# A three-layer interaction network with gathered embeddings: scales without rounding to powers of two, and embedding gathers spread two to a step

## The reference

```python
B, F, E = (1024, 48, 32)
LAYER_SIZES = [128, 128, 128]

def _cin_layer(xi, x0, W, b):
    Fi, F0 = (xi.shape[1], x0.shape[1])
    Wr = W.reshape(Fi, F0, -1)
    out = jnp.einsum('nie,nje,ijo->noe', xi, x0, Wr) + b[None, :, None]
    return jax.nn.relu(out)
```

## Time and profile before

| | us |
|---|---|
| median of 3 runs | 2438.37 |
| lowest and highest of them | 2435.81, 2439.48 |
| the profiled execution, its own time | 2440.96 |
| its span, from first to last instruction | 2439.2 |
| PE busy | 2319.3 (95%) |
| DVE busy | 2267.9 (93%) |
| ACT busy | 2115.5 (87%) |
| POOL busy | 1954.1 (80%) |

### The profile page before, as it was taken

The page is one execution under the profiler, slowest core; times in us unless marked ns, Lnnn a source line. Parts: engine busy times, 40 slices in busy tenths (PEclk is TensorE's granted clock), DMA queues, the critical chain, the costliest instruction groups (busy, mean ns, idle before and its releaser), DMA issues.

```text
span 2439.2 us, 68108 instructions
## 1 busy us (share of the span) xinstructions
PE 2319.3 (95%) x14174; PEld 1183.7 (49%) x14174; DVE 2267.9 (93%) x9416; ACT 2115.5 (87%) x7910; POOL 1954.1 (80%) x2134
## 2 busy tenths in 40 slices
PE   1699999999999999999999999999999999999999
PEld 0355455454455454555445544544445555555453
DVE  6499999999999999999999999999999999999995
ACT  4589889888889889889889889889889999999895
POOL 7588888888888888888888888888777777777774
PEclk6799999999999999999999999999999999999999
DMA  5133333333333333333333333333333333333331
GB/s 170 28 72 70 64 70 71 64 68 71 61 71 71 64 68 71 68 66 69 68 65 70 70 71 63 70 71 66 65 70 68 69 63 71 69 69 71 69 70 30
DMA packets 150185, 168.19 MB, mean 69 GB/s; under 512 B 111940, under 2 KB 115655, under 8 KB 150120
## 3 DMA queue, kind: packets, MB, share of 16 engines
q0 software_dynamic: 42864, 136.87, 30.1%
q1 hardware_dynamic: 107256, 30.73, 5.8%
HBM read 12.82 MB, written 0.00 MB: 5 GB/s over the span
## 4 chain that ended last, share of the span: by engine, by line
PE 30%; POOL 18%; issue 16%; ACT 13%; DMA 11%; DVE 9%; DVEq 1%; SPq 1%; ACTq 1%; POOLq 0%
PE y L509 25%; DMA work<-work 10%; ACT work L623 8%; DVE acc L843 5%; POOL part L355 5%; PE m L499 3%; POOL part L359 3%; POOL part L357 3%; POOL emb L300 2%; ACT work L653 2%; POOL psum L362 2%; POOL rest L347 1%; POOL work L332 1%; DVEq L96 1%; ACT zh L651 1%
## 5 line engine op out<-in xcount | busy, mean ns | idle before, releaser
L509 PE MATMUL y<-whi,xT 128*128 128x512 f16 x6144 | 2000.5, 380 | 39.8 <-DVE acc L843 34.0
L623 ACT ACTIVATE work<-y,xc 128x128 f32<-128x128 f32 x5632 | 1610.0, 419 | 182.5 <-PE y L509 158.2
L843 DVE SCALAR_TENSOR_TENSOR acc<-y,xc,acc 128x128 f32<-128x128 f32 x5632 | 1657.6, 346 | 32.0 <-PE y L509 26.3
L509 PE MATMUL y<-wlo,xT 128*128 128x512 f16 x3072 | 1165.6, 379 | 0.0
L509 PEld LDWEIGHTS y<-whi,xT 128*128 128x128 f16 x6144 | 599.3, 98 | 679.9 <-issue 73.6
L509 PEld LDWEIGHTS y<-wlo,xT 128*128 128x128 f16 x3072 | 300.9, 98 | 230.3 <-issue 0.7
L355 POOL TENSOR_TENSOR part<-work 128x512 f32<-128x512 f32 x255 | 324.5, 1272 | 84.4 <-DMA work<-work 68.7
L384 POOL TENSOR_TENSOR zl<-work,zh 128x1152 f16<-128x1152 f32 x128 | 343.3, 2682 | 8.1 <-ACT work L653 8.1
L332 POOL DMA_DIRECT2D work<-work x255 | 229.1, 898 | 111.4 <-ACT work L623 110.2
L343 POOL TENSOR_TENSOR part<-work 128x512 f32<-128x512 f32 x128 | 164.4, 1284 | 133.0 <-ACT work L623 132.9
L300 POOL DMA_INDIRECT emb<-tbl,ids_sb x192 | 202.0, 1052 | 46.7 <-issue 44.2
(11 more groups left out here) (108 smaller groups left out, 2098.8 us busy)
## 6 DMA issues: line engine op xcount, KB each, us to landing
work<-work POOLq DMA_DIRECT2D x255, 512.0 KB, 4.8
xT<-hi SPq DMA_TRANSPOSE x256, 2.2
xT<-lo SPq DMA_TRANSPOSE x256, 2.2
emb<-tbl,ids_sb POOLq DMA_INDIRECT x192, 2.5
xx<-w SPq DMA_DIRECT2D x4, 768.0 KB
work<-w SPq DMA_DIRECT2D x4, 768.0 KB
x0T<-x0hl SPq DMA_TRANSPOSE x128, 2.2
wt_sb<-W_top SPq DMA_DIRECT2D x1, 768.0 KB
```

Of the source, the lines that this page charges most:

```text
L509: ins = nc.tensor.matmul(dst[:], xT[layer][:, parity, a, :], w[layer][:, cols], start=i == 0, stop=i == 2)
L623: nc.scalar.activation(prods[layer][:, a, k * P:(k + 1) * P], bank[:, k * P:(k + 1) * P], ACT.Copy, scale=xc[layer][:, parity, j:j + 1]).t ...
L843: ins = nc.vector.scalar_tensor_tensor(dst, y, col, mine, ALU.mult, ALU.add)
```

## The change

It has three parts.

1. **Scales.** The exponent masking is left out, so that scales are no longer powers of two: `scale` becomes two instructions (`tot`, `sc`) and `x0_scale` three. ACT reads `tot` where it read `mpw`. The factor `wpow` is put into the embeddings themselves when they are spread: `tensor_copy` becomes `tensor_scalar` with `wpow`, on DVE for block 0 and on POOL for the others. ACT's `mpsq` divides it out again with `scale=winv`.
2. **Layout.** In `mx0` the maximum and the clipped maximum of a tile now stand side by side, so the instructions on the two tiles read and write with a stride of two elements.
3. **Gathers.** From step 1 on every step has two gathers, until step 68, where the 144 are given out. The spreads stand in steps 21 to 24, 45 to 48 and 69 to 72.

```diff
-SPREAD, GROUP, EARLY = 8, 12, 8
+SPREAD, GROUP = 8, 12
-SCALE = 4
+SCALE, SCALE0 = 2, 4
...
-                pool.tensor_copy(xx[:, t0:t0 + n, :], src).then_inc(s_xx, n)
+                pool.tensor_scalar(xx[:, t0:t0 + n, :], src, wpow[:, 0:1], None, ALU.mult).then_inc(s_xx, n)
...
-                if v > 0 and (parity == 1 or v <= EARLY):
+                if v > 0:
                     next_gather()
...
-                nc.scalar.activation(mpsq[:], mp0[:], ACT.Square).then_inc(s_mpsq, 2)
+                nc.scalar.activation(mpsq[:], mx0[:, :, 1], ACT.Square, scale=winv[:, 0:1]).then_inc(s_mpsq, 2)
...
-                wait(act, s_scale[l], t * SCALE + 4)
+                wait(act, s_scale[l], (t + 1) * SCALE)
...
-                                     ACT.Copy, scale=mpw[l][:]).then_inc(s_xc[l], 1)
+                                     ACT.Copy, scale=tot[l][:, 1:2]).then_inc(s_xc[l], 1)
...
-                    nc.vector.tensor_scalar(mx0[:, 1, :], mx0[:, 0, :], TINY0, HALF_RANGE, ALU.max, ALU.mult).then_inc(s, 1)
-                elif i == 2:
                     wait(dve, s, done + 2)
                     wait(dve, s_msq, t)
-                    nc.vector.tensor_scalar(mp0[:].bitcast(u32), mx0[:, 1, :].bitcast(u32), EXPONENT, None,
-                                            ALU.bitwise_and).then_inc(s, 1)
-                else:
+                    nc.vector.tensor_scalar(mx0[:, :, 1], mx0[:, :, 0], TINY0, HALF_RANGE, ALU.max, ALU.mult).then_inc(s, 1)
+                elif i == 2:
                     wait(dve, s, done + 3)
                     wait(dve, s_xs0, t)
-                    nc.vector.reciprocal(sc0[:], mp0[:]).then_inc(s, 1)
+                    nc.vector.reciprocal(sc0[:], mx0[:, :, 1]).then_inc(s, 1)
...
                 elif i == 1:
                     wait(dve, s, done + 1)
-                    nc.vector.tensor_scalar(mp[l][:].bitcast(u32), tot[l][:, 1:2].bitcast(u32), EXPONENT, None,
-                                            ALU.bitwise_and).then_inc(s, 1)
-                elif i == 2:
-                    wait(dve, s, done + 2)
                     wait(dve, s_hi[l], t)
-                    nc.vector.reciprocal(sc[l][:], mp[l][:]).then_inc(s, 1)
-                else:
-                    wait(dve, s_xc[l], t)
-                    nc.vector.tensor_scalar(mpw[l][:], mp[l][:], wpow[:, 0:1], None, ALU.mult).then_inc(s, 1)
+                    nc.vector.reciprocal(sc[l][:], tot[l][:, 1:2]).then_inc(s, 1)
```

More of the change, by code:

```diff
@@ L74 @@
 TINY = 1e-30
-TINY0 = 1e-15
+TINY0 = 1e-20
 EXPONENT = 0x7F800000
@@ L120, in build @@
         mx0, sc0 = sb("mx0", [P, 2, 2]), sb("sc0", [P, 2])
-        mp0, mpsq, msq = sb("mp0", [P, 2]), sb("mpsq", [P, 2]), sb("msq", [P, 2])
+        mpsq, msq = sb("mpsq", [P, 2]), sb("msq", [P, 2])
         whi = [sb(f"whi{l}", [P, F * P], f16) for l in (2, 3)]
@@ L144, in build @@
         tot = [sb(f"tot{l}", [P, 2]) for l in (1, 2)]
-        mp = [sb(f"mp{l}", [P, 1]) for l in (1, 2)]
-        mpw = [sb(f"mpw{l}", [P, 1]) for l in (1, 2)]
         sc = [sb(f"sc{l}", [P, 1]) for l in (1, 2)]
@@ L386, in x0_scaled @@
             def x0_scaled(t):
-                wait(pool, s_x0, t * 2 + SCALE)
+                wait(pool, s_x0, t * 2 + SCALE0)
                 wait(pool, s_x0lo, t)
@@ L786, in spread @@
                 fields = slice(g * GROUP, (g + 1) * GROUP)
-                return nc.vector.tensor_copy(xx[:, e0:e1, fields], emb[:, 0, fields, e0:e1].rearrange("p f e -> p e f"))
+                return nc.vector.tensor_scalar(xx[:, e0:e1, fields], emb[:, 0, fields, e0:e1].rearrange("p f e -> p e f"),
+                                               wpow[:, 0:1], None, ALU.mult)
             for g in range(F // GROUP - 1):
@@ L801, in x0_scale @@
                     wait(dve, s_xx, t + 2)
-                    nc.vector.tensor_reduce(mx0[:, 0, :], xx[:, bass.ds(t, 2), :], axis=AX.X, op=ALU.max,
-                                            apply_absolute_value=True).then_inc(s, 1)
+                    nc.vector.tensor_reduce(mx0[:, :, 0], xx[:, bass.ds(t, 2), :], axis=AX.X, op=ALU.max,
+                                            apply_absolute_value=True).then_inc(s, 2)
                 elif i == 1:
-                    wait(dve, s, done + 1)
-                    nc.vector.tensor_scalar(mx0[:, 1, :], mx0[:, 0, :], TINY0, HALF_RANGE, ALU.max, ALU.mult).then_inc(s, 1)
-                elif i == 2:
                     wait(dve, s, done + 2)
                     wait(dve, s_msq, t)
-                    nc.vector.tensor_scalar(mp0[:].bitcast(u32), mx0[:, 1, :].bitcast(u32), EXPONENT, None,
-                                            ALU.bitwise_and).then_inc(s, 1)
-                else:
+                    nc.vector.tensor_scalar(mx0[:, :, 1], mx0[:, :, 0], TINY0, HALF_RANGE, ALU.max, ALU.mult).then_inc(s, 1)
+                elif i == 2:
                     wait(dve, s, done + 3)
                     wait(dve, s_xs0, t)
-                    nc.vector.reciprocal(sc0[:], mp0[:]).then_inc(s, 1)
+                    nc.vector.reciprocal(sc0[:], mx0[:, :, 1]).then_inc(s, 1)
             def stacked_lo(t):
@@ L871, in scale @@
                     wait(dve, s_relu[l], t + 1)
+                    wait(dve, s_xc[l], t)
                     nc.vector.tensor_scalar(tot[l][:, 1:2], tot[l][:, 0:1], TINY, HALF_RANGE, ALU.max,
@@ L920, in step @@
                             pre1(t1, parity)
-                        if n == 7 and active(t1):
+                        if n == 7 and k < SCALE and active(t1):
                             scale(0, t1, k)
@@ L935, in step @@
                             stacked_lo(t1 + 1)
-                        if n == 23 and active(t2):
-                            scale(1, t2, k)
+                        if n == 23 and k in (1, 3) and active(t2):
+                            scale(1, t2, k // 2)
                     if n == 14 and isinstance(v, int) and TILES - 3 - NB * PIECES <= v < TILES - 3:
```

## The result

| kernel | median us | lowest to highest | ratio to before, 95% interval |
|---|---|---|---|
| before | 2438.18 | 2435.81 to 2439.48 | |
| changed | 2422.43 | 2420.61 to 2422.9 | 0.9936, 0.9921 to 0.9951 |

The change takes off 15.8 us; 10.5 were forecast. The profiled execution of the changed kernel took 2422.4 us.

What follows compares the result with a forecast made beforehand. PE was taken to set the pace without gathers (35.36 us a pair), a 36.22 us loop with them; terms -7.7 + 3.0 - 2.7 - 3.6 + 1.2 - 0.7 = -10.5 us gave 2427.9 us, range 2410 to 2440.

Steps and rivals of the forecast that it cites:

- Fewer steps with gathers: Gathers end at step 68, not 88; ten pairs fall to PE's pace, 0.77 us each: -7.7 us.
- A second gather in even steps: Even steps 10 to 68, between `x0_scaled` and `sum_rest(0)`: 30 added gathers at 0.1 us, +3.0 us; bounds 0 and 0.14.
- the cover: POOL's wait for ACT ahead of `sum_rest(0)`, 1.64 us, hides the added gather, with 0.42 us left.
- second rival: If ACT comes over 0.42 us earlier against POOL, the even-step gather is exposed: 37 us more, 2462 us; chance 0.08.
- The earlier release of `hi_part`: ACT's wait for `mpw` shrinks: 0.08 us in each of 34 gather pairs, -2.7 us; bounds 0 and 0.19 us.
- L810 and `mpw` in spread steps: Six even steps with a spread, where DVE's instructions are uncovered: 0.6 us saved each, -3.6 us; bounds nothing and -8.4.
- the spreads' multiplication: POOL's twelve spreads as `tensor_scalar` instead of copy: +0.1 us each, +1.2 us in all; bounds 0 and +19 us.
- Start and end: Scale chains at the first and last tiles have no cover, so shorter scales save there: -0.7 us.
- The loop: Gather stage, closing once a pair through POOL, DVE, PE, ACT: 36.22 us; only shortening its terms shortens the pair, until 35.36.
- POOL's leg: From `add_by_dma(1)` to the end of `psum`: 17.52 us, 16.35 without gathers; the gather behind `squares_lo` makes the difference.
- Its signs: Named trace marks: gather-stage pairs of 36.1 to 36.2 us, POOL's ACT wait about 0.4, spreads 0.9 to 1.1 us.
- The full opening: DVE savings count in full and the gather stage runs at PE's pace: 42 us less, 2396 us; chance 0.1.

Runs made afterwards that it cites:

- e2: Changed kernel with the gathers as before (two and one by turns behind step 8), so scales and spreads alone: 2423.82 us, ratio 0.9938.
- e1: Kernel before with two gathers in every step from step 1 on and nothing else: 2429.7 us, ratio 0.9959.
- e6: Kernel before with one wait moved: layer 1's `hi_part` waits for the third scale instruction, not the fourth: 2429.61 us, ratio 0.9964.
- e3: Changed kernel with POOL's spreads as plain copies, leaving out `wpow` on blocks 1 to 3: 2416.02 us, ratio 0.9901.
- e5: Changed kernel, but behind step 8 the gather behind `squares_lo` is given out in odd steps alone: 2423.09 us, ratio 0.9931.
- e10: Changed kernel with block 1 gathered at the start, then one gather a step, ahead of `sum_rest(0)`, from step 1 on: 2458.94 us, one execution.
- e7: Changed kernel with four small DVE instructions a step put back, writing to a tile nobody reads or waits for: 2422.31 us, ratio 0.9935.

## Why the prediction was right, and where it was not

**The two parts together.** By the terms, the scales with their spreads were to give 5.8 us and the gathers 4.7, together 10.5. Alone they gave 16 (e2) and 10 (e1), and both at once 15.8. Both were forecast too low, by 10 and by 5 us, and they overlap by 10 us, which the sum, where each term stands as if alone, left out. The forecast lies as near as it does because the overlap took back most of what the terms lacked. That is luck.

**Fewer steps with gathers (-7.7 us).** With the old scales -11.3 us (e1, one profile), with the new ones -4.2, since there a pair is worth 0.40 and not 0.77 us.

**A second gather in even steps (+3.0 us).** With the old scales 0 (e1), the lower bound, and the cover was as described. With the new ones 4.6 us, of which the terms on ACT gave no sign: ACT was to gain 0.19 us at most, and the 0.43 us of wait that e1 shows are gone in the changed kernel. So the second rival's condition came, but not its price of 37 us: POOL waits for the adding DMA behind the gather anyway, so 0.15 us a gather was paid and not 1.24, about what that DMA's later landing takes.

**The earlier release of `hi_part` (-2.7 us).** The mechanism was right and the size too small. The release alone gives 0.18 us a pair (e6) where 0.08 was taken, 7.5 us in all. The 1.25 us of the stage without gathers were taken as ACT's own time, and they contained a wait: the same stretch takes 1.01 us once `hi_part` does not wait. The bound of 0.19 us, the idle time shown, was also too small for ACT's stretch, which fell by 0.32: back to back, the end of the products overlaps the start of `hi_part` by 1308.67 + 1.14 - 1309.68 = 0.13 us, and a wait uses up this overlap before any idle time shows. For the pair, though, 0.18 us lies within the bound. That this is not the whole of what the scales give is seen in e2's 0.40 us, and the prediction has no term for the rest.

**L810 and `mpw` in spread steps (-3.6 us), the spreads' multiplication (+1.2 us).** The second was mis-sized: 0.755 us each in place of 0.1, inside the bounds, and 6 to 8.5 us of the 9.1 on the path (e3). The values nearest in kind, tensor_tensor of plain operands, were the wrong guide. L806 was stopped as before, longer now, since the spread is longer. What the first term gave by itself was not measured.

**Start and end (-0.7 us).** Of the right kind, and twice the size: the first tiles are 0.67 us earlier, and from the last `squares_lo` to the end it takes 2420.5 - 2348.89 = 71.61 us in place of 2439.2 - 2366.72 = 72.48.

**The loop.** In the kernel before, its place, its legs and PE's wait were right. One thing in POOL's leg was read too simply: the second gather, called off the path, stands beside an adding DMA that lands 1302.95 - 1297.65 = 5.30 us after its issue, and without gathers, where POOL does not wait for that DMA, the same sum starts 1917.47 - 1912.53 = 4.94 us after it. So 0.36 us of the difference of 1.17 us lie there and not at the first gather. That it was the only one was wrong, and with that the sentence that what shortens a leg shortens the pair: e6 made ACT's way to `hi_part` 0.36 us shorter and the pair 0.18. Two such chains stand side by side. The old scales leave the late `psum` to the odd steps, the new ones to the even steps; relieving the chain that ends in the odd steps' `psum` then did nothing (e5), and with both relieved the pairs take PE's 35.36 us (e10).

**Its signs.** Pairs of 36.1 to 36.2 us in the gather stage were named, and 36.0 came. A wait of 0.4 us for ACT in even steps was named, and none was left. The spread was to take 0.9 to 1.1 us, and took 1.73. DVE's share in the full stage was to fall by some 3 points, and fell from 97.62 to 96.36 between 1900 and 2000 us. The full opening did not come, and the part of DVE's relief that e7 took back was worth nothing, as argued.

## What to carry to other kernels

Before pricing a cut in a loop of waits, look for a second loop offset by one step: here a cut in one of them stopped paying as soon as the other set the pace. Price parts of a change on top of each other and not each alone. An engine's queue has covered and uncovered places, and what is covered hangs on when the engine it waits for comes; giving the spreads the place of a covered gather, and such steps no gathers, was worth about as much as the whole change. Ask which instruction a consumer's semaphore waits for before asking how many the producer has. And take the pace from many pairs: one pair of the changed kernel shows 35.77 us where the usual one has 36.0.

## What was not expected of the hardware

- POOL's tensor_scalar with a pointer took 1.73 us for 384 elements a partition, the copy of the same operands 0.98 us.
- A gather issued beside an adding DMA made that DMA land 0.1 to 0.2 us later (5.13 to 5.27 us in e5 and 5.12 to 5.44 in the changed kernel, against 5.04 to 5.08 in e2).
- ACT's stretch from the first of four products to `hi_part` showed 1.25 us with no idle time, and took 1.01 us once the wait in it was gone: in the timeline an instruction overlaps the one before it by 0.13 us, and a shorter wait does not show as idle time.
